# A four-layer residual network on one core: the fourth norm's residual taken out of the routing stage, weighings in three pairs, and smaller moves

## The reference

```python
x = x + attention(_layernorm(x))         # 16 heads of 8, softmax over 256 keys, biases
x = x + recurrence(_layernorm(x))        # c = ft * c + it * gt over time, then tanh
x = x + linear_attention(_layernorm(x))  # rotary, elu + 1, 16 heads of 8
x = x + experts(_layernorm(x))           # 16 experts, top 2, hidden 256, exact gelu
# the last one, with xt = _layernorm(x):
w, idx = jax.lax.top_k(softmax(xt @ Wr + br), 2); w = w / sum(w)
y = xt + sum over the two experts of w * (gelu(xt @ W1 + b1) @ W2 + b2)
```

## Time and profile before

| | us |
|---|---|
| median of 3 runs (605.43 to 611.54) | 610.13 |
| the profiled execution's own time | 609.49 |
| its span, first to last instruction | 607.7 |
| PE, DVE, ACT, POOL busy | 497.6, 411.7, 344.0, 361.9 |
| mean granted clock of TensorE, share of full speed | 0.917 |

### The profile page before, as it was taken

One profiled execution on the slowest core, in us unless ns is written; L12 is line 12 of the kernel. 1 busy time (PEld: TensorE's weight loads), 2 busy tenths in 40 slices (PEclk: granted clock), 3 DMA queues, 4 the chain that ended last, 5 costly groups with the idle time before them and its releaser, 6 DMA issues. The chain is left out here.

```text
span 607.7 us, 14282 instructions
## 1 busy us (share of the span) xinstructions
PE 497.6 (82%) x4164; PEld 334.2 (55%) x4164; DVE 411.7 (68%) x1070; ACT 344.0 (57%) x733; POOL 361.9 (60%) x605
## 2 busy tenths in 40 slices
PE   4757889999999999998877888888764899899800
PEld 3523445555555555444555566665544798888800
DVE  6776868888788888872235899999757255545206
ACT  2026767777777777667524677766531476555500
POOL 3555777777777777533230177777564277777750
PEclk8769999999999999999987999998655999999965
DMA  3667443433333433300044011111114333333229
GB/s 104 173 166 194 117 112 87 113 103 101 105 89 97 108 97 104 109 4 5 1 141 144 1 37 36 37 41 35 32 37 110 81 94 95 95 96 91 72 78 344
DMA packets 66460, 55.97 MB, mean 92 GB/s; under 512 B 8523, under 2 KB 59872, under 8 KB 66400
## 3 DMA queue, kind: packets, MB, share of 16 engines
q1 hardware_dynamic: 58584, 45.13, 27.5%
q0 software_dynamic: 4608, 8.47, 4.2%
q10 hardware_dynamic: 3208, 1.65, 1.1%
HBM read 30.54 MB, written 25.71 MB: 93 GB/s over the span
## 5 line engine op out<-in xcount | busy, mean ns | idle before, releaser
L456 DVE TENSOR_REDUCE negmax<-p_dve 128x4 f32<-128x1024 f32 x128 | 156.2, 1223 | 46.7 <-PE p_dve L682 45.0
L574 ACT ACTIVATE probs<-p_exp 128x1024 f32<-128x1024 f32 x128 | 130.7, 1021 | 29.5 <-PE p_exp L656 29.0
L1633 POOL DMA_INDIRECT back<-XN2T,rows x80 | 82.2, 1028 | 40.1 <-issue 22.6
L1117 POOL DMA_INDIRECT disp<-pay,pos x64 | 69.6, 1087 | 32.2 <-DVE pos L1316 18.5
L673 PE MATMUL p_out<-probs,V 128*32 128x256 f32 x1024 | 75.2, 388 | 0.0
L656 PE MATMUL p_exp<-QS,KS 64*128 64x256 bf16 x512 | 50.6, 276 | 11.2 <-ACT probs L574 5.8
L682 PE MATMUL p_dve<-KS,QS 61*128 61x256 bf16 x512 | 51.2, 280 | 9.8 <-DVE negmax L456 9.7
L1723 ACT ACTIVATE hid<-p_qkv,own 128x128 f32<-128x128 f32 x160 | 45.6, 368 | 22.4 <-PE p_qkv L1763 19.0
L1763 PE MATMUL p_qkv<-XN2T,own 128*128 128x128 f32 x320 | 43.0, 277 | 2.5 <-ACT XN2T L1713 2.5
L1687 DVE COPY own<-expert 128x578 f32 x80 | 35.5, 487 | 11.4 <-issue 11.1
L1763 PEld LDWEIGHTS p_qkv<-XN2T,own 128*128 128x128 f32 x320 | 38.8, 191 | 3.6 <-ACT XN2T L1713 3.4
(11 more groups left out here) (267 smaller groups left out, 1212.8 us busy)
## 6 DMA issues: line engine op xcount, KB each, us to landing
scratch<-part SPq DMA_DIRECT2D x32, 192.0 KB, 2.1
KS<-scratch SPq DMA_DIRECT2D x32, 192.0 KB, 3.2
QS<-scratch SPq DMA_DIRECT2D x32, 192.0 KB, 4.2
rows<-disp SPq DMA_DIRECT2D x80, 65.0 KB
scratch<-part SPq DMA_DIRECT2D x32, 128.0 KB, 1.9
own<-back SPq DMA_DIRECT2D x8, 512.0 KB, 6.4
expert<-in_W_dram SPq DMA_DIRECT2D x1, 2064.0 KB, 8.8
scratch<-part SPq DMA_DIRECT2D x32, 64.0 KB, 1.8
```

The lines of the kernel that those rows point to most:

```text
L456: dve.tensor_reduce(negmax[q][:, i, :, 2 * hp:2 * hp + 2], p_dve[buf][:, :].rearrange("p (v w k) -> p v w k", v=HALF, k=S), AX.X, ALU.max, ...
L574: act.activation(probs[s % 4][:, :, :, :].rearrange("p v w q -> p (v w q)"), p_exp[:, :], ACT.Exp)\
L1117: pool.indirect_dma_start(out=disp, out_offset=bass.IndirectOffsetOnAxis(ap=pos[q][:, i, k:k + 1], axis=0), in_=pay[q][:, k, i, :], in_off ...
L1633: pool.indirect_dma_start(out=back, out_offset=bass.IndirectOffsetOnAxis(ap=rows[r][:, h, D + 1:ROW].bitcast(U32), axis=0), in_=y[r][:, h, :],
```

## The change

- **Residual of the fourth norm.** `X += pay` (L1319) goes. ACT copies scale and shift of each block (`kept`, 128x4) as the first operation of its iteration, waiting for `nw`. In the expert stage, after the copies of tile 4's experts (`LATE_NORM`), DVE adds 1 to the scales and makes `X * (scale + 1) + shift` in 32 operations of 128x128.
- **One sum for places and counts.** `place` is 48 wide: 32 ranks and 16 counts, added to the count in the last block's `place`. The sum `nup` goes.
- **Weighings.** `WEIGHED_IN` has three slots with two units each. Before, five slots held 1, 1, 2, 1, 1.
- **Iteration 1 of the first stage.** SP writes parts 3 and 4 after the transfer of row maxima, not before it; PE's turn of keys and queries goes from slot 1 to slot 2, and its scores for ACT ahead of the maxima in slot 4. `setup()` on POOL goes from iteration 3 to 2.
- **Token layout.** Two neighbouring tokens lie in one partition, in the loads of `x` and the store of the result (packets of 1 KB); `cosf` and `sinf` are loaded in two pieces each to suit.
- **Start of the experts.** `IDLE_TURNS` is 18, not 30, and PE makes 10 single matmuls (`IDLE_AT_PLAN`) before it waits for the plan. Of the eight pairs of pads SP fills three and ACT five, where each had four. SP loads the first table entry before it waits for the scatters, not behind them.

The diff, cut to what follows from these points:

```diff
-WEIGHED_IN = {2: (0,), 3: (1,), 4: (2, 3), 6: (4,), 7: (5,)}
+WEIGHED_IN = {2: (0, 1), 4: (2, 3), 6: (4, 5)}
...
-                if at(n, 3):
+                if at(n, 2):
                     setup()
...
-                if s == 1 and active(n, -1):
+                if s == (2 if at(n, 1) else 1) and active(n, -1):
...
+                    if s == 4 and at(n, 1):
+                        for_act(n, r, s)
...
-IDLE_TURNS = 30
+IDLE_AT_PLAN = 10
+IDLE_TURNS = 18
+LATE_NORM = 4
...
-            fill_pads(sp, 0)
+            fill_pads(sp, (0, 2, 4))
...
-                    ranks = p_r[:, 64:64 + TT * E].rearrange("p (i e) -> p i e", i=TT)
-                    dve.tensor_tensor(place[:, :, :], ranks, wide(nup[o][:, :].rearrange("p (o e) -> p o e", o=1), [P, TT, E]), ALU.add)\
+                    ranks = p_r[:, 64:64 + (TT + 1) * E].rearrange("p (i e) -> p i e", i=TT + 1)
+                    taken = place[(b - 1) % PAIR][:, TT, :] if b else count[:, :]
+                    if b:
+                        dve.wait_ge(pos_s.sem, pos_s.at(b - 1, 1))
+                    dve.tensor_tensor(place[b % PAIR][:, :, :], ranks, wide(taken.rearrange("p (o e) -> p o e", o=1), [P, TT + 1, E]), ALU.add)\
                         .then_inc(pos_s.sem, 1)
...
-                if active(n, 5):
-                    dve.tensor_tensor(nup[r][:, :], p_r[:, 96:96 + E], nup[o][:, :], ALU.add).then_inc(pos_s.sem, 1)
...
-                if active(n, 5):
-                    b = n - 5
-                    dve.tensor_tensor(X[:, bass.ds(2 * b, 2), :], X[:, bass.ds(2 * b, 2), :], pay[b % STORED][:, 0, :, 0:D], ALU.add).then_inc(res.sem, 1)
...
             def iteration(n, r):
                 o = 1 - r
+                if active(n, 5):
+                    b = n - 5
+                    act.wait_ge(nw.sem, nw.at(b + 3))
+                    act.activation(kept[:, b, :, :], root[r][:, 0:3:2, TT:2 * TT], ACT.Copy).then_inc(kept_s.sem, 1)
...
-            fill_pads(act, 1)
+            fill_pads(act, (1, 3, 5, 7, 6))
...
+            pe.wait_ge(o_s.sem, o_s.at(B - 1))
+            for _ in range(IDLE_AT_PLAN):
+                pe.matmul(p_kvo[:, 0:P], ident[:, :], ident[:, :], start=True, stop=True)
...
-        for q in range(STORED):
-            sp.wait_ge(t["sent"][q].sem, t["sent"][q].at((B - 1 - q) // STORED))
-        sp.wait_ge(w["loaded3"].sem, w["loaded3"].at(0))
-        sp.wait_ge(pads_first.sem, pads_first.at(0))
         sp.wait_ge(table.sem, 1)
...
             word = sp.value_load(tablei[0:1, 1, bass.ds(2 * i, 1)], min_val=0, max_val=(1 << 2 * PLACE_BITS) - 1)
+            if isinstance(i, int) and i == 0:
+                sp.wait_ge(w["loaded3"].sem, w["loaded3"].at(0))
+                sp.wait_ge(pads_first.sem, pads_first.at(0))
+                for q in range(STORED):
+                    sp.wait_ge(t["sent"][q].sem, t["sent"][q].at((B - 1 - q) // STORED))
...
-        ov = t["out"].rearrange("(n p) d -> p n d", p=P)
+        ov = t["out"].rearrange("(b p i) d -> p b (i d)", p=P, i=TT)
...
+            if isinstance(i, int) and i == LATE_NORM:
+                dve.tensor_scalar(t["kept"][:, :, 0, :], t["kept"][:, :, 0, :], 1.0, None, ALU.add).then_inc(up_s.sem, 1)
+                dve.wait_ge(up_s.sem, up_s.at(0))
+                for n in range(2 * B):
+                    b, one = divmod(n, TT)
+                    dve.tensor_scalar(X[:, n, :], X[:, n, :], t["kept"][:, b, 0, one:one + 1], t["kept"][:, b, 1, one:one + 1], ALU.mult, ALU.add)\
+                        .then_inc(res.sem, 1)
```

More of the change, by code:

```diff
@@ L310, in iteration @@
                     sp.dma_start(max_rows.rearrange("i h t -> (i h) t"), maxT[:, :]).then_inc(maxrow_out.sem, 16)
-                if active(n, -1):
+                if active(n, -1) and not at(n, 1):
                     write_parts(n + 1, (r + 1) % RING, 3, ((1, 0, 3, 5), (0, 1, 3, 5)))
@@ L321, in iteration @@
                         sp.dma_start(QS[q][row:row + PARTS, :, :], max_rows[:, u * H // HALF:(u + 1) * H // HALF, :]).then_inc(maxrow_in.sem, 16)
+                if active(n, -1) and at(n, 1):
+                    write_parts(n + 1, (r + 1) % RING, 3, ((1, 0, 3, 5), (0, 1, 3, 5)))
+                    write_parts(n + 1, (r + 1) % RING, 4, ((1, 0, 0, 3), (0, 2, 5, 6)))
                 if active(n, -1):
@@ L878, in iteration @@
                     else:
-                        for_act(n, r, s)
+                        if not (s == 4 and at(n, 1)):
+                            for_act(n, r, s)
                         for_dve(n, r, s)
@@ L930, in linear_attention_and_routing @@
         mv, root = [tmp(f"mv_{r}", [P, 2 * TT, 3]) for r in range(PAIR)], [tmp(f"root_{r}", [P, 4, 2 * TT]) for r in range(PAIR)]
+        kept = t["kept"] = tmp("kept", [P, B, 2, TT])
         xn3 = [tmp(f"xn3_{r}", [P, TT, D]) for r in range(PAIR)]
@@ L946, in linear_attention_and_routing @@
         sel = [tmp(f"sel_{r}", [P, 2 + TT, E], BF16) for r in range(PAIR)]
-        place, mine = tmp("place", [P, TT, E]), tmp("mine", [P, TT, TOP, E])
+        place, mine = [tmp(f"place_{r}", [P, TT + 1, E]) for r in range(PAIR)], tmp("mine", [P, TT, TOP, E])
         pos = [tmp(f"pos_{r}", [P, TT, TOP], U32) for r in range(STORED)]
-        nup = [count, tmp("count_b", [P, E])]
+        counts = place[(B - 1) % PAIR][:, TT, :]
         p_h, p_ta, p_tb, p_qkv = psum("p_h"), psum("p_ta"), psum("p_tb"), psum("p_qkv", 1024)
@@ L1000, in plan_tiles @@
             dve.wait_ge(pos_s.sem, pos_s.at(B - 1))
-            then(dve.tensor_tensor(full[:, :], count[:, :], w["region"][:, :], ALU.subtract))
+            then(dve.tensor_tensor(full[:, :], counts, w["region"][:, :], ALU.subtract))
             then(dve.tensor_copy(endi[:, :], full[:, :]))
@@ L1039, in plan_tiles, with fill_pads @@
             dve.tensor_copy(tablei[:, :, :], tablef[:, :, 0:TILES]).then_inc(table.sem, 1)
-        def fill_pads(eng, q):
+        def fill_pads(eng, pairs):
             eng.wait_ge(plan.sem, plan.at(0, 4))
             eng.wait_ge(fill_set.sem, fill_set.at(0))
-            for pair in range(q, E // 2, 2):
+            for pair in pairs:
                 word = eng.value_load(endi[0:1, 2 * pair:2 * pair + 1], min_val=0, max_val=(TOKENS << END_BITS) + TOKENS)
@@ L1051, in fill_pads @@
                     eng.dma_start(disp[bass.ds(place, P), :], w["fill"][:, :])\
[L1052 removed]
+                        .then_inc(pads_first.sem if pair < FIRST_PADS // 2 else pads[pair % 2].sem, 16)
         def banks_free(pe):
```

55 lines of the change are left out of this document (29 added, 26 removed).

## The result

The changed kernel takes **614.58 us** (median of 20 runs, 611.52 to 620.35), the kernel before 609.59 (20 runs beside them, 604.38 to 612.74). The ratio is 1.010, 95% interval 1.0076 to 1.0124: slower, by 5.0 us. The forecast was 614.7.

What follows compares the result with a forecast made beforehand. DVE, busy 98%, was taken as tied within 0.03 us with chains through ACT's `rl` and POOL's power operation. Terms 9.6 − 1.7 − 0.4 + 0 − 1.3 + 0 − 1.0 = +5.2 on 609.5 gave 614.7 us, range 602 to 621.

Steps and rivals of the forecast that it cites:

- `kept` at the head of ACT's iteration makes `feat` late: Linear attention: ACT's copy waits for the shift and delays `xn`, `rl` and `feat`; +0.70 us per iteration, +9.6 in all.
- DVE's removed work is worth nothing: Linear attention: at most 0.59 us per iteration leaves DVE, which would then only wait at `feat` for ACT's `rl`.
- rival B: Linear attention: DVE is the bound, `kept` falls in slack, 11 iterations lose 0.41 us each; 600.6 us, chance 0.10.
- Rival C, the clock in the second stage: Second stage: PE's clock falls and lengthens iterations by 0.45 us, 5 us in all; 619.7 us, chance 0.15.
- Weighings, 0: First stage: merging weighings on PE into three slots changes nothing; 0 us, range −5.9 to +2.9.
- the ring: First stage: PE, ACT and DVE wait for one another in turn across the slots, so merged weighings gain 0.
- Rival D: First stage: the merged weighings gain two thirds of their bound, −3.9 us; 610.8 us, chance 0.10.
- `setup()`, −1.7: First stage: moving POOL's `setup()` to iteration 2 hides it and removes PE's wait in iteration 3; −1.7 us.
- Iteration 1, −0.4: First stage: the row-maxima transfer, moved ahead of two writes on SP's queue, comes sooner for PE; −0.4 us (−1.6 to +1.6).
- Start of the experts, −1.3: Expert stage: with fewer idle turns PE is free before the rows land and starts real turns sooner; −1.3 us (−2.5 to 0).
- Late norm, 0: Expert stage: DVE's lump, at most 11.4 us, makes two tiles' first sums up to 2 us late, absorbed; 0 us.
- Writes in 1 KB, −1.0: Final writes: eight writes take 0.63 us each and not 0.76, at the reads' rate of 419 GB/s; −1.0 us.

Runs made afterwards that it cites:

- e2: The kernel before with only the copy `kept` added at the head of ACT's iteration; ratio to the kernel before 1.0117, 649.34 us beside 644.8.
- e1: The changed kernel with `kept` moved on ACT to just ahead of `pay`; ratio to the kernel before 0.9965, 642.09 us beside 644.8.
- e9: The changed kernel without any copy of scale and shift, each block's root in its own slice; 606.54 us beside 609.04, ratio to the kernel before 0.9966.
- e3: The changed kernel with the weighings dealt to five slots as before; ratio to the kernel before 1.0023.
- e4: The changed kernel with `setup()` on POOL back in iteration 3; ratio to the kernel before 1.005.
- e11: The changed kernel with no copy, the late norm behind the expert loop, and iteration 1 in the old order; 606.99 us, ratio to the kernel before 0.9951.
- e5: The changed kernel run again, unaltered, as control for its set; ratio to the kernel before 1.0036, 648.05 us.
- e7: The changed kernel with the old start of the experts (30 idle turns, no idle matmuls before the plan, old pads and table load); ratio to the kernel before 1.0043.
- e10: The changed kernel with the late norm moved behind the loop over expert tiles; 617.53 us, ratio to the kernel before 1.0127.
- e12: The kernel before, profiled a second time with nothing changed; 604.24 us.

## Why the prediction was right, step by step

The time came out, 614.58 for 614.7, and the mechanism of its largest term is shown. Much of that nearness is luck, since errors of single terms cancel: `kept` was priced 2.9 us too high, iteration 1 has the wrong sign, the start of the experts, `setup()` and the writes give less than forecast, and the longer tail of the first stage was not in the sum.

- *`kept` at the head of ACT's iteration makes `feat` late.* Right. Adding it alone gives a period of 7.78 (e2), moving it alone takes the period from 7.85 to 7.40 (e1), removing it gives 7.34 (e9). The size was too high: +0.70 forecast, +0.56 measured. The term for `kept` itself was mis-sized. It was priced at 0.24 by `odds` and holds ACT for 0.11 from start to start (382.74 to 382.85), and `odds` held it 0.37 and not 0.48, since 0.1 of those 0.48 were `xn`'s wait for the shift, which ended at 389.69. So `xn` came 0.78 later and not 0.99. Over the stage it is +6.7 instead of +9.6. Half of the 2.9 between is this size, 11 x 0.14; the other half the ramp and the drain, for which I had 1.9 and which come to about 0.5 (6.7 less 11 x 0.56). DVE's share fell to 90% and not to 85%.
- *DVE's removed work is worth nothing.* Right, and shown without the copy: 7.34 with it removed (e9), 7.31 before, as means. Beside ACT's `rl` a third arrival binds, which I had not named: PE's product for `X<-p_u`, for which DVE waits 0.22 to 0.46. So rival B is out. The Trainium skill (Perfetto Trace Analysis, Identifying the Most-Contended Engine) takes the engine with the highest occupancy for the bottleneck; DVE's was 98%, and 0.5 us off it changed the period by +0.03.
- *Rival C, the clock in the second stage.* Out. The granted clock from 360 to 420 is 1.00 with PE busy 49.81 of 60 us (83%), where it was 52.41.
- *Weighings, 0.* Right for the steady part, where the argument of the ring holds: 171.6 or 171.7 us with five slots, 170.9 to 171.8 with three (e3). Rival D is out. The ring says nothing of the ramp and the drain. There three slots are about 1 us shorter and 2 us longer, the latter by PE's wait for POOL's `xn` and the fall of the clock behind it; that both together come near 0 is luck.
- *`setup()`, −1.7.* Right in kind; 1.3 by e4.
- *Iteration 1, −0.4.* Wrong in sign. From the first row maximum to the 17th the kernel before takes 27.3 and 27.5 us, the changed one 28.1 and 28.6; e11, with the old order, takes 27.7. The transfer QS<-max_rows hardly came sooner: it is issued 3.0 us behind that of the maxima (37.90 and 40.90), before 3.2 (36.50 and 39.71), since it waits for that one to land and not for the queue. The two writes behind it became later; that these are what costs is argued and not shown. I had priced the wait on PE and not asked what SP was waiting for.
- *Start of the experts, −1.3.* To the first scatter −0.8 and −0.1 against the two profiles of before, −1.2 for e5 against e7, and not to be seen in the times. In e5 the real turns start 3.0 us sooner than in e7, and the late norm then holds the first sum.
- *Late norm, 0.* The lump takes 8.29 us and ends on the first tile's sum (490.38 and 490.30), so it is a cover that had no room left. It was priced at up to 11.4 us. I had it ending up to 2 us late and absorbed; in e5 the sum is 1.8 late, so that bound was right. It is not absorbed there up to the first scatter: of the 3.0 us that the start wins in e5 it takes back 1.8.
- *Writes in 1 KB, −1.0.* 382 GB/s, so 0.69 us a piece instead of 0.76, −0.6 by rate and −0.4 in the stretch. The Trainium skill (DMA: Bandwidth & Descriptors, Specifications) would have 512 bytes enough for line rate. Here writes in packets of 1 KB run 11% faster than the same writes in 512 bytes, so neither that nor the rate of the reads was right.

The parts in the profiles don't add up to the medians exactly. The second stage gives +6.7 and the last stretch −0.4. The first stage from first maximum to its end gives +0.6 (mean of e1, e5, e7, e9 and e10, 295.3, less that of before, e2 and e12, 294.7), and the start of the experts between −0.8 and −0.1. That is +6.1 to +6.8, beside +5.0 by the medians and about +2.3 by the ratio of e5. The difference is open.

## What to carry to other kernels

Here an operation of 0.1 us cost 0.5 us in every iteration, as it was put ahead of work that used to fill the wait it brings. Ask what stands behind a new wait in the queue, not how long the operation is. An engine that is busy 98% need not be the bound: look whether its inputs arrive with a margin, and where two chains arrive within hundredths of a microsecond, taking work from the engine between them bought nothing here. Look at the first and the last iterations of a pipeline too: a merging that changes nothing in the steady part made the drain 2 us longer. When a copy is made to keep something from being overwritten, a buffer for each block can take its place at no cost in time (e9).
